# Gate weights of a low-rank expert layer spread by DMA within SBUF instead of by a matmul, with h left in PSUM

## Chip, cores and metric

One core of one Trainium2 chip runs the whole kernel. The metric is the time of one execution on the device in microseconds (us), as the median over several executions. The engines are named as in the profile: PE is TensorE's matmul side and PEld its weight loads, DVE is VectorE, ACT is ScalarE, POOL is GpSimd, SP is the engine that only issues DMAs here.

## The reference

All of it is float32. 64 batches of 64 tokens with 512 features go through a conditioned layer and then through a feed-forward layer with low-rank experts:

```
q_emb = relu(cond @ W3 + b3)                       # (64, 512)
x1    = (64 * x + sum_over_tokens(x)) * q_emb      # (64, 64, 512)  (n is x.shape[1] = 64)
y     = relu(x1 @ W2 + b2)
base  = y @ W_base + b_base
shared = (y @ A_s) @ B_s                           # rank 16
gates = softmax(y @ W_router + b_router)           # 6 experts
w     = gates where among the top 2 of the token, else 0
h     = y @ A_r                                    # per expert, rank 16
routed = sum over experts of (h * w) @ B_r
out   = x + base + shared + routed
```

## The kernel before

The 4096 tokens are cut into NG = 8 groups of TG = 512 tokens (TT = 4 tiles of 128 tokens; KC = 4 chunks of 128 features). Every large product is made in three passes of a format with fewer bits: each operand is split into hi and lo, and hi*hi, hi*lo and lo*hi are added up in PSUM (`product`, L658 to L663, whose matmuls all carry L661).

For a group there are these stages. **Turn and total** (DVE): the load in quarters x_quart is transposed to xT (`turn_x`, L420), summed over the tokens of a batch (`sum_x`, L426) and added (`add_sum`, L432). POOL multiplies by q_emb (`scale`, L277) into x1_full, ACT rounds to x1_hi (`x1_split`, L318) and DVE makes x1_lo (`x1_rest`, L443). **m1** (PE, L665): four outputs of 12 matmuls, y before the relu. ACT makes y_full and y_hi (`relu`, L323), DVE y_lo (`y_rest`, L449). **h** (PE, L705): 12 matmuls into the PSUM bank hT. One product gives all low-rank rows at once: rows 0 to 5 are the router's logits, row 6 (ONE) is empty and gets its 1 from a bias, rows 16 to 31 (SH) are the shared expert's, rows 32 to 127 (RO on) are 6 experts x 16. **m2** (PE, L719): 48 matmuls of y with W_base into four banks m2_ps, tokens on partitions. **Gates**: ACT copies the logits' rows out of hT (h_head, L394) and evacuates all of hT with its bias to h_sb (L398); DVE turns the logits so that tokens stand on partitions, and ranks the experts (`rank_experts`, L476); ACT takes the exponential; DVE divides the two largest by the sum (`gates`, L505) and transposes the result back (wT, L522). **Expand**: ACT copies wT's four quarters to the four diagonal blocks of w_quads (`w_spread`, L359 to L364), and one matmul with the constant 0/1 matrix pick writes, over h in the bank hT, the weight of each row and token (`expand`, L742 to L748). So that the weights lose nothing in the format with fewer bits, w_pack holds each of them as hi and lo in two columns (L516 to L520), and pick adds the two; a column of ones feeds the rows 0 to 31. DVE multiplies (`weigh`, L524 to L532): hw_full = hT * h_sb. ACT rounds to hw_hi (`hw_split`, L366) and DVE makes hw_lo (`hw_rest`, L534). **up** (PE, L729): 12 matmuls of hw with B into the four banks of m2; DVE adds x (`add_x`, L540, instructions at L548) and SP stores.

The order of each engine is written out by hand in a `step(g, par)` for each, the groups interleaved; semaphores alone tie the engines together. PE (L759 on): in step g >= 1 expand(g-1), m1 of outputs 0 and 1, up for group g-1, m1 of outputs 2 and 3, then h and m2 of group g. In the last step expand(7) stands before the last three products of m2, and up in two halves follows. DVE (L551 on): in a step g >= 2 it turns chunk 0 of group g+1, then weigh(g-1), total of chunk 0, hw_rest, y_rest(0) and so on, and near the end rank_experts(g), gates(g) and the last two x1_rest. In the first two steps the order differs: turn(3) and total(3) stand behind gates. The first step g=0 uses `m1_first` (L678). In the last step weigh, hw_split and hw_rest run over halves of 256 tokens.

h of the next group waits until weigh has read hT (`hw_ready`, L711 to L712). weigh waits for h_ready (h_sb) and gates_done (expand); expand waits for h_ready and for w_quads_ready.

SP's queue in step g (L231 to L239) is: wait until the four chunks of group g are turned, load the quarters of group g+2 (L205); store the four tiles of group g-1 as each becomes ready (L229); load x_nat of group g+1 (L239). ACT and POOL issue no DMA in the steps.

The semaphore count that the gates use is GATE_STEPS = 11 a group. Before the steps, POOL builds w_pack's zeros, w_quads' zeros and pick_one (L263 to L275), and ACT copies pick_one to the four blocks of pick (L355 to L357), behind the rounding of W_base and ahead of the first relu.

## Time and profile before

| what | value |
|---|---|
| median of 3 runs | 247.85 us (246.45 to 248.17) |
| the profiled execution | 246.59 us |
| its span, first to last instruction | 244.9 us |
| mean granted TensorE clock in it | 0.979 of full speed |

The profile is of one execution. Its span is what all stretches and waits below are parts of; the time around it is the rest up to 246.59 us. A time in a row is counted from the start of the span.

### The profile page before, as it was taken

How to read it: one execution, taken by the hardware profiler on the slowest of the kernel's cores; microseconds unless marked ns; L12 is line 12 of the kernel's file. 1: busy time of each engine (PE TensorE's matmuls, PEld its weight loads, DVE VectorE, ACT ScalarE, POOL GpSimd, SP SyncE). 2: the span in 40 equal slices, each digit the busy share in tenths (PEclk: the TensorE clock that was granted, in tenths of full speed). 3: DMA queues.
4: the chain of work that ended last, by engine and by line, in shares of the span. 5: the costliest groups of instructions: out<-in, count | busy, mean ns of one | idle time of the engine just before them, and what ended most of it. 6: DMA issues, size and time to landing. Idle time of an engine off the chain costs nothing.

```text
span 244.9 us, 3159 instructions
## 1 busy us (share of the span) xinstructions
PE 235.0 (96%) x1007; PEld 189.4 (77%) x1007; DVE 177.4 (72%) x324; ACT 102.1 (42%) x206; POOL 55.7 (23%) x58
## 2 busy tenths in 40 slices
PE   7699599999999999999999999999999999999994
PEld 2577378888887878888888888888888888888883
DVE  0697898869988996679766995679756995351344
ACT  2247557234434445245533455145433455134330
POOL 5078971202312041012302121012202121000000
PEclk9769979999999999999999999999999999999999
DMA  7989990818016368019610567018000530013004
GB/s 151 299 198 208 270 249 1 170 69 280 0 58 116 146 200 171 0 43 299 143 33 0 183 197 137 0 43 300 0 0 0 192 150 0 0 53 120 3 0 173
DMA packets 32219, 28.49 MB, mean 116 GB/s; under 512 B 6173, under 2 KB 22621, under 8 KB 32206
## 3 DMA queue, kind: packets, MB, share of 16 engines
q1 hardware_dynamic: 32050, 28.33, 42.9%
q8 instruction: 6, 0.10, 0.2%
q14 instruction: 7, 0.06, 0.1%
q10 hardware_dynamic: 156, 0.00, 0.0%
HBM read 19.94 MB, written 8.39 MB: 116 GB/s over the span
## 4 chain that ended last, share of the span: by engine, by line
PE 69%; DVE 16%; SPq 6%; DMA 4%; issue 2%; POOL 1%; ACT 1%; POOLq 0%; DVEq 0%
PE m_ps L661 61%; PE hT L661 7%; DMA x_quart<-in_x_dram 4%; DVE xT L424 4%; DVE out_nat L548 3%; DVE x_sum L438 3%; SPq L217 2%; DVE vsum L429 2%; DVE y_lo L452 2%; SPq L205 1%; POOL x_full L284 1%; DVE x_lo L446 1%; SPq L211 1%; PE hT L748 1%; ACT x_hi L321 1%
## 5 line engine op out<-in xcount | busy, mean ns | idle before, releaser
L284 POOL TENSOR_TENSOR x_full<-x_sum,qT 128x512 f32<-128x512 f32 x31 | 37.9, 1222 | 138.5 <-DVE x_sum L438 138.5
L661 PE MATMUL m_ps<-Wb_lo,y_hi 128*128 128x512 f32 x128 | 50.1, 391 | 0.0
L661 PE MATMUL m_ps<-Wb_hi,y_lo 128*128 128x512 f32 x128 | 50.1, 391 | 0.0
L661 PE MATMUL m_ps<-Wb_hi,y_hi 128*128 128x512 f32 x128 | 50.0, 391 | 0.0
L661 PE MATMUL m_ps<-x_hi,W_hi 128*128 128x512 f32 x112 | 43.8, 391 | 0.2 <-DVE x_lo L446 0.2
L661 PE MATMUL m_ps<-x_lo,W_hi 128*128 128x512 f32 x112 | 43.6, 389 | 0.0
L661 PE MATMUL m_ps<-x_hi,W_lo 128*128 128x512 f32 x112 | 43.6, 389 | 0.0
L329 ACT ACTIVATE y_full<-m_ps,b_sb 128x512 f32<-128x512 f32 x32 | 22.0, 688 | 49.3 <-PE m_ps L661 46.4
L424 DVE STREAM_TRANSPOSE xT<-x_quart 128x512 f32<-128x512 f32 x32 | 34.8, 1088 | 7.6 <-DMA x_quart<-in_x_dram 7.6
L452 DVE TENSOR_TENSOR y_lo<-y_full,y_hi 128x512 fp32r<-128x512 f32 x32 | 25.0, 780 | 12.5 <-ACT y_hi L331 12.5
L446 DVE TENSOR_TENSOR x_lo<-x_full,x_hi 128x512 fp32r<-128x512 f32 x32 | 22.9, 719 | 10.9 <-ACT x_hi L321 10.9
L321 ACT ACTIVATE x_hi<-x_full 128x512 fp32r<-128x512 f32 x32 | 20.1, 632 | 22.2 <-POOL x_full L284 21.4
L661 PEld LDWEIGHTS m_ps<-Wb_hi,y_hi 128*128 128x128 f32 x128 | 24.3, 190 | 5.0
L661 PEld LDWEIGHTS m_ps<-Wb_lo,y_hi 128*128 128x128 f32 x128 | 24.2, 189 | 5.1
L661 PEld LDWEIGHTS m_ps<-Wb_hi,y_lo 128*128 128x128 f32 x128 | 24.2, 189 | 5.1
L438 DVE SCALAR_TENSOR_TENSOR x_sum<-xT,vsum 128x512 f32<-128x512 f32 x32 | 24.8, 774 | 2.1
L661 PEld LDWEIGHTS m_ps<-x_hi,W_hi 128*128 128x128 f32 x112 | 21.0, 188 | 5.2 <-DVE x_lo L446 0.9
L548 DVE TENSOR_TENSOR out_nat<-m_ps,x_nat 128x512 f32<-128x512 f32 x32 | 20.6, 683 | 5.5 <-PE m_ps L661 5.5
L661 PEld LDWEIGHTS m_ps<-x_hi,W_lo 128*128 128x128 f32 x112 | 21.0, 188 | 4.4
L661 PEld LDWEIGHTS m_ps<-x_lo,W_hi 128*128 128x128 f32 x112 | 21.0, 188 | 4.3
L429 DVE TENSOR_REDUCE vsum<-xT 128x8 f32<-128x512 f32 x32 | 21.8, 680 | 0.3
L331 ACT ACTIVATE y_hi<-m_ps,b_sb 128x512 fp32r<-128x512 f32 x32 | 21.8, 682 | 0.0
(82 smaller groups left out, 263.7 us busy)
## 6 DMA issues: line engine op xcount, KB each, us to landing
x_quart<-in_x_dram SPq DMA_DIRECT2D x32, 256.0 KB, 4.8
x_nat<-in_x_dram SPq DMA_DIRECT2D x8, 1024.0 KB, 6.0
out_dram<-out_nat SPq DMA_DIRECT2D x32, 256.0 KB, 2.1
W_f<-in_L_cond_W_dram SPq DMA_DIRECT2D x4, 256.0 KB, 6.3
Wb_f<-in_L_ffn_W_base_dram SPq DMA_DIRECT2D x1, 1024.0 KB, 7.0
W_sb<-in_L_cond_W_dram SPq DMA_DIRECT2D x1, 512.0 KB, 6.0
Wd_f<-in_L_ffn_A_r_dram SPq DMA_DIRECT2D x4, 48.0 KB, 3.1
Wu_f<-in_L_ffn_B_r_dram SPq DMA_DIRECT2D x1, 192.0 KB
```

The source lines that it names most:

```text
L217: sp.dma_start(Wd_f[:, k, RO:P].rearrange("p (e r) -> p e r", r=R), A_r[:, k * P:(k + 1) * P, :].rearrange("e p r -> p e r")).then_inc(Wd_ ...
L284: nc.gpsimd.tensor_tensor(per_batch(x1_full[:, c, :]), per_batch(x1_sum[:, c, :]), qT[:, c, bass.ds(BG * g, BG)].unsqueeze(2).to_broadcast ...
L321: nc.scalar.activation(x1_hi[par][:, c, :], x1_full[:, c, :], ACT.Copy).then_inc(x1_hi_ready, 1)
L329: nc.scalar.activation(y_full[m % 2][:, :], m1_ps[m][:, :], ACT.Relu, bias=b2_sb[:, m:m + 1]).then_inc(y_full_ready, 1)
L331: nc.scalar.activation(y_hi[:, m, :], m1_ps[m][:, :], ACT.Relu, bias=b2_sb[:, m:m + 1]).then_inc(y_hi_ready, 1)
L424: nc.vector.transpose(xT[c % 2][:, :], x_quart[par][:, :, :].rearrange("p b (i c) -> p c b i", c=KC)[:, c]).then_inc(xT_ready, 1)
L429: nc.vector.tensor_reduce(vsum[c % 2][:, :], per_batch(xT[c % 2][:, :]), AX.X, ALU.add).then_inc(vsum_ready, 1)
L438: nc.vector.scalar_tensor_tensor(out=per_batch(x1_sum[:, c, :]), in0=per_batch(xT[c % 2][:, :]), scalar=float(N), in1=vsum[c % 2][:, :].un ...
L446: nc.vector.tensor_tensor(x1_lo[par][:, c, :], x1_full[:, c, :], x1_hi[par][:, c, :].bitcast(F32), ALU.subtract).then_inc(x1_lo_ready, 1)
L452: nc.vector.tensor_tensor(y_lo[:, m, :], y_full[m % 2][:, :], y_hi[:, m, :].bitcast(F32), ALU.subtract).then_inc(y_lo_ready, 1)
L548: nc.vector.tensor_tensor(out_nat[par][:, t, :], m2_ps[t][:, :], x_nat[par][:, t, :], ALU.add).then_inc(out_ready, 1)
L661: mm = nc.tensor.matmul(psum, lhsT, rhs, start=start and i == 0, stop=stop and i == len(terms) - 1)
```

## The change

The weights reach the rows of h without TensorE. DVE writes them once, in float32, to w_nat (no hi and lo, no column of ones) and transposes to wT as before. SP then issues four DMAs, one for each quarter of the tokens, from six partitions of wT to the 96 partitions 32 to 127 of the new tile gatesT, each source row read 16 times. Rows 0 to 31 of gatesT are set to 1.0 once by POOL. In SP's step the four issues stand last, behind a wait for wT, so ahead of the next step's load of quarters. `weigh` waits for all four and adds the bias and multiplies in one instruction, hw_full = (hT + h_bias) * gatesT, reading h from PSUM; h_sb is gone, and so are w_full, the hi/lo packing, w_quads, pick, expand and what built them. GATE_STEPS is 9. The diff, without most of the declarations:

```diff
-        w_full = sb("w_full", [P, TT, E])
-        w_pack = sb("w_pack", [P, TT, S], F32R)
+        w_nat = sb("w_nat", [P, TT, S])
...
-        w_quads = sb("w_quads", [P, TG], F32R)
-        pick_one = sb("pick_one", [S, P])
-        pick = sb("pick", [P, P], F32R)
+        gatesT = sb("gatesT", [P, TG])
...
-        GATE_STEPS = 11
+        GATE_STEPS = 9
 
         block = ctx.enter_context(nc.Block())
 
@@ -237,6 +232,10 @@
                     store(g - 1, 1 - par)
                 if not (isinstance(g, int) and g + 1 >= NG):
                     sp.dma_start(x_nat[1 - par][:, :, :], at(x_groups, g + 1)).then_inc(x_loaded[1 - par], 16)
+                sp.wait_ge(wT_ready, g + 1)
+                for q in range(NQ):
+                    spread = wT[q * S:q * S + E, :].unsqueeze(1).to_broadcast([E, R, P])
+                    sp.dma_start(gatesT[RO:P, q * P:(q + 1) * P], spread).then_inc(gates_spread, 16)
 
             step(0, 0, first=True)
             with sp.Fori(0, (NG - 4) // 2) as pair:
@@ -260,19 +259,8 @@
 
             nc.gpsimd.affine_select(out=earlier[:, :, :], in_=earlier[:, :, :], compare_op=ALU.is_gt, fill=0.0,
                                     base=0, pattern=[[1, E], [-1, E]], channel_multiplier=0).then_inc(const_ready, 1)
-            nc.gpsimd.memset(w_pack[:, :, :].bitcast(F32), 0.0).then_inc(pick_step, 1)
-            nc.gpsimd.memset(pick_one[:, :], 0.0).then_inc(pick_step, 1)
-            nc.gpsimd.memset(w_quads[:, :].bitcast(F32), 0.0).then_inc(const_ready, 1)
-            pool.wait_ge(pick_step, 2)
-            nc.gpsimd.memset(w_pack[:, :, 2 * E:2 * E + 1].bitcast(F32), 1.0).then_inc(const_ready, 1)
-            experts = pick_one[:, RO:P].rearrange("p (e r) -> p e r", r=R)
-            nc.gpsimd.affine_select(out=experts, in_=experts, compare_op=ALU.not_equal, fill=1.0,
-                                    base=0, pattern=[[-1, E], [0, R]], channel_multiplier=1).then_inc(pick_step, 1)
-            nc.gpsimd.affine_select(out=pick_one[:, 0:RO], in_=pick_one[:, 0:RO], compare_op=ALU.not_equal, fill=1.0,
-                                    base=-2 * E, pattern=[[0, RO]], channel_multiplier=1).then_inc(pick_step, 1)
-            pool.wait_ge(pick_step, 4)
-            nc.gpsimd.affine_select(out=experts, in_=experts, compare_op=ALU.not_equal, fill=1.0,
-                                    base=-E, pattern=[[-1, E], [0, R]], channel_multiplier=1).then_inc(pick_step, 1)
+            nc.gpsimd.memset(w_nat[:, :, :], 0.0).then_inc(const_ready, 1)
+            nc.gpsimd.memset(gatesT[0:RO, :], 1.0).then_inc(const_ready, 1)
 
             def scale(g, c):
 
@@ -352,17 +340,6 @@
             act.wait_ge(b2_loaded, 16)
             act.wait_ge(bias_loaded, 16)
 
-            act.wait_ge(pick_step, 5)
-            for q in range(NQ):
-                nc.scalar.activation(pick[q * S:(q + 1) * S, :], pick_one[:, :], ACT.Copy).then_inc(pick_ready, 1)
-
-            def w_spread(g):
-
-                act.wait_ge(wT_ready, g + 1)
-                for q in range(NQ):
-                    nc.scalar.activation(w_quads[q * S:(q + 1) * S, q * P:(q + 1) * P], wT[q * S:(q + 1) * S, :],
-                                         ACT.Copy).then_inc(w_quads_ready, 1)
-
             def hw_split(toks, n):
 
                 act.wait_ge(hw_ready, n)
@@ -393,9 +370,6 @@
                 for q in range(NQ):
                     nc.scalar.activation(h_head[q * S:(q + 1) * S, :], hT[0:S, q * P:(q + 1) * P], ACT.Identity,
                                          bias=h_bias[0:S, 0:1]).then_inc(h_head_ready, 1)
-                if not first:
-                    act.wait_ge(hw_ready, g)
-                nc.scalar.activation(h_sb[:, :], hT[:, :], ACT.Identity, bias=h_bias[:, 0:1]).then_inc(h_ready, 1)
                 if first:
                     split(0)
                     split(1)
@@ -405,7 +379,6 @@
                 nc.scalar.activation(expo[:, :, :], logit[:, :, :], ACT.Exp).then_inc(expo_ready, 1)
                 if first:
                     split(2)
-                w_spread(g)
                 split(3)
                 if last:
                     hw_split(slice(0, TG // 2), g + 1)
@@ -513,13 +486,9 @@
                 nc.vector.reciprocal(rden[:, :], den[:, :]).then_inc(gate_step, 1)
                 dve.wait_ge(gate_step, done + 9)
                 top, norm = expo_top[:, :, :], rden[:, :].unsqueeze(2).to_broadcast([P, TT, E])
-                nc.vector.tensor_tensor(w_full[:, :, :], top, norm, ALU.mult).then_inc(gate_step, 1)
-                nc.vector.tensor_tensor(w_pack[:, :, 0:E], top, norm, ALU.mult).then_inc(gate_step, 1)
-                dve.wait_ge(gate_step, done + 11)
-                nc.vector.tensor_tensor(w_pack[:, :, E:2 * E], w_full[:, :, :], w_pack[:, :, 0:E].bitcast(F32),
-                                        ALU.subtract).then_inc(w_ready, 1)
+                nc.vector.tensor_tensor(w_nat[:, :, 0:E], top, norm, ALU.mult).then_inc(w_ready, 1)
                 dve.wait_ge(w_ready, g + 1)
-                nc.vector.transpose(wT[:, :], w_pack[:, :, :].bitcast(F32).rearrange("p t j -> p (t j)")).then_inc(wT_ready, 1)
+                nc.vector.transpose(wT[:, :], w_nat[:, :, :].rearrange("p t j -> p (t j)")).then_inc(wT_ready, 1)
 
             def weigh(g, toks, n):
 
@@ -527,9 +496,9 @@
                     dve.wait_ge(hw_hi_ready, g)
                 if isinstance(g, int) and g == NG - 1:
                     dve.wait_ge(hw_hi_ready, NG - 1)
-                dve.wait_ge(h_ready, g + 1)
-                dve.wait_ge(gates_done, g + 1)
-                nc.vector.tensor_tensor(hw_full[:, toks], hT[:, toks], h_sb[:, toks], ALU.mult).then_inc(hw_ready, 1)
+                dve.wait_ge(gates_spread, 16 * NQ * (g + 1))
+                nc.vector.scalar_tensor_tensor(out=hw_full[:, toks], in0=hT[:, toks], scalar=h_bias[:, 0:1],
+                                               in1=gatesT[:, toks], op0=ALU.add, op1=ALU.mult).then_inc(hw_ready, 1)
 
             def hw_rest(toks, n):
 
@@ -739,14 +708,6 @@
                     product(m2_ps[t][:, :], [(hw_lo[:, toks], Wu_hi[:, :])], False, True).then_inc(m2_done, 1)
 
 
-            def expand(g):
-
-                if isinstance(g, int) and g == 0:
-                    pe.wait_ge(pick_ready, NQ)
-                pe.wait_ge(h_ready, g + 1)
-                pe.wait_ge(w_quads_ready, NQ * (g + 1))
-                nc.tensor.matmul(hT[:, :], pick[:, :], w_quads[:, :], start=True, stop=True).then_inc(gates_done, 1)
-
             pe.wait_ge(W3_loaded, 16)
             pe.wait_ge(condT_copied, 1)
             for c in range(KC):
@@ -761,7 +722,6 @@
                 if first:
                     m1_first()
                 else:
-                    expand(g - 1)
                     m1(g, par, 0)
                     m1(g, par, 1)
                     up(range(TT), g)
@@ -790,7 +750,6 @@
 
                     for t, k in others[:-3]:
                         m2(t, k, first)
-                    expand(g)
                     for t, k in others[-3:]:
                         m2(t, k, first)
                     up(range(TT // 2), g + 1)
```

## Rows read from the trace of the kernel before

**Rows 1.** Page, part 1: busy us (share of the span) xinstructions of each engine

```profile
PE 235.0 (96%) x1007; PEld 189.4 (77%) x1007; DVE 177.4 (72%) x324; ACT 102.1 (42%) x206; POOL 55.7 (23%) x58
```

**Rows 2.** Waits of all engines: who waited for whom, us in total, times, longest

```profile
DVE hw_full L532 <- PE hT L748: 9.9, 6, 2.9
...
PE hT L661 <- DVE y_lo L452: 2.9, 2, 2.7
```

**Rows 3.** Windows: stretch, length, busy us of each engine, granted clock, DMA share

```profile
core 0: us, PE busy (x) PEld busy (x) DVE busy (x) ACT busy (x) POOL busy (x), PEclk, DMA share, GB/s
30.40:33.50 3.10, 3.10 (x7) 2.46 (x8) 3.10 (x5) 2.65 (x5) 2.52 (x2) 0.50 1.20 215
45.30:72.70 27.40, 27.40 (x122) 22.52 (x121) 23.98 (x41) 11.48 (x23) 3.94 (x4) 1.00 0.40 111
72.70:101.20 28.50, 28.04 (x123) 22.56 (x122) 23.29 (x43) 12.11 (x24) 5.85 (x5) 1.00 0.57 145
```

**Rows 4.** Chain that ended last, in order of time: start us, us, what

```profile
101.51 13.60 PE m_ps L661 x60
```

**Rows 5.** Groups by form: line engine op out<-in shapes xcount | busy, mean ns | idle before

```profile
L438 DVE SCALAR_TENSOR_TENSOR x_sum<-xT,vsum 128x512 f32<-128x512 f32 x32 | 24.8, 774 | 2.1
...
L532 DVE TENSOR_TENSOR hw_full<-hT,h_sb 128x512 f32<-128x512 f32 x7 | 4.8, 685 | 7.0 <-PE hT L748 7.0
...
L748 PE MATMUL hT<-w_quads,pick 128*128 128x512 f32 x8 | 3.1, 389 | 0.0
```

**Rows 6.** Timeline of the last step: start us, us, engine, line, op, out<-in [idle before]

```profile
233.00 0.18 DVE L516 TENSOR_TENSOR w_full<-expo_top,rden 128x24 f32<-128x24 f32 x1
...
233.10 0.18 DVE L517 TENSOR_TENSOR w_pack<-expo_top,rden 128x24 fp32r<-128x24 f32 x1
...
233.31 0.18 DVE L519 TENSOR_TENSOR w_pack<-w_full,w_pack 128x24 fp32r<-128x24 f32 x1
...
233.53 0.31 DVE L522 STREAM_TRANSPOSE wT<-w_pack 128x128 f32<-128x128 f32 x1
...
236.74 0.76 DVE L532 TENSOR_TENSOR hw_full<-hT,h_sb 128x256 f32<-128x256 f32 x2 [2.89 <-PE hT L748]
...
237.19 0.75 ACT L369 ACTIVATE hw_hi<-hw_full 128x256 fp32r<-128x256 f32 x2 [2.01 <-DVE hw_full L532]
...
237.64 0.76 DVE L537 TENSOR_TENSOR hw_lo<-hw_full,hw_hi 128x256 fp32r<-128x256 f32 x2 [0.15 <-ACT hw_hi L369]
...
238.48 0.39 PE L661 MATMUL m_ps<-Wu_hi,hw_hi 128*128 128x512 f32 x1
```

**Rows 7.** Timeline of PE at the two places where it stopped in step 2

```profile
74.66 0.39 PE L661 MATMUL m_ps<-x_hi,W_lo 128*128 128x512 f32 x1
75.27 0.50 PE L661 MATMUL m_ps<-x_hi,W_hi 128*128 128x512 f32 x1 [0.22 <-DVE x_lo L446]
...
90.59 0.39 PE L661 MATMUL hT<-y_hi,Wd_lo 128*128 128x512 f32 x1
91.22 0.50 PE L661 MATMUL hT<-y_lo,Wd_hi 128*128 128x512 f32 x1 [0.24 <-DVE y_lo L452]
```

**Rows 8.** Timeline of a steady step, from wT to the first matmul of up

```profile
178.69 0.32 DVE L522 STREAM_TRANSPOSE wT<-w_pack 128x128 f32<-128x128 f32 x1
...
183.92 0.69 DVE L532 TENSOR_TENSOR hw_full<-hT,h_sb 128x512 f32<-128x512 f32 x1 [1.21 <-PE hT L748]
...
185.94 0.68 DVE L537 TENSOR_TENSOR hw_lo<-hw_full,hw_hi 128x512 fp32r<-128x512 f32 x1
...
189.06 0.39 PE L661 MATMUL m_ps<-Wu_hi,hw_hi 128*128 128x512 f32 x1
```

**Rows 9.** SP's DMA issues: timeline of one; landing times of L229, then of L205

```profile
43.14 1.94 SPq L205 DMA_DIRECT2D x_quart<-in_x_dram  x4
...
DMA to landing us min/median/max: 2.0/2.1/2.6
...
DMA to landing us min/median/max: 3.0/4.8/10.5
```

**Rows 10.** Page, part 3: DMA queue, kind: packets, MB, share of 16 engines

```profile
q1 hardware_dynamic: 32050, 28.33, 42.9%
```

More of the change, by code:

```diff
@@ L79, in adaln_ffn @@
         y_lo = sb("y_lo", [P, KC, TG], F32R)
-        h_sb = sb("h_sb", [P, TG])
         h_head = sb("h_head", [P, P])
@@ L154, in adaln_ffn @@
         m1_done, y_full_ready, y_hi_ready, y_lo_ready = sem("m1_done"), sem("y_full_ready"), sem("y_hi_ready"), sem("y_lo_ready")
-        h_done, h_ready = sem("h_done"), sem("h_ready")
+        h_done = sem("h_done")
         h_head_ready, logit_ready, expo_ready, gate_step = sem("h_head_ready"), sem("logit_ready"), sem("expo_ready"), sem("gate_step")
-        w_ready, wT_ready, w_quads_ready, gates_done = sem("w_ready"), sem("wT_ready"), sem("w_quads_ready"), sem("gates_done")
-        pick_step, pick_ready = sem("pick_step"), sem("pick_ready")
+        w_ready, wT_ready, gates_spread = sem("w_ready"), sem("wT_ready"), sem("gates_spread")
         hw_ready, hw_hi_ready, hw_lo_ready = sem("hw_ready"), sem("hw_hi_ready"), sem("hw_lo_ready")
         m2_done, out_ready = sem("m2_done"), sem("out_ready")
-        GATE_STEPS = 11
+        GATE_STEPS = 9
         block = ctx.enter_context(nc.Block())
```

## The prediction, made before the changed kernel was run

> **What bounds the kernel now.** I read the busy line of the page first, then the waits, then the stages in windows, the chain, and last the timeline at the three places where the change bites. TensorE is busy for 96% of the span [rows 1]. Of the waits that stop it the largest in the steps are two on y_lo, 2.9 us together with 2.7 in one of them [rows 2]. The long one lies near 27 to 30 us, before the first expand. In the windows of the steps, TensorE is busy for 27.40 of 27.40 us in step 1 and for 28.04 of 28.50 in step 2 [rows 3]. From there on the chain is one unbroken run of matmuls: 60 in 13.60 us, 0.227 us from start to start [rows 4]. (The 389 ns of one matmul in the groups is its length in the pipeline, not its price.) A full step is 48 matmuls of m1, 12 of up, 12 of h, 48 of m2 and one expand: 121 x 0.227 = 27.4 us, which is what the window of step 1 shows. So from about 33 us to 239 us the time is the number of matmuls times 0.227, plus small stalls in step 2. VectorE (72%) and ScalarE (42%) count only where TensorE waits for them.
>
> **What the change takes from TensorE.** Eight expand matmuls, one for each group [rows 5]: 8 x 0.227 = 1.81 us. Seven stand at the head of a step and one in the last step among the last products of m2. All lie on the path, for nothing stops the engine before or behind them.
>
> **What it takes from VectorE.** gates loses w_full and the subtraction into w_pack. In the last step w_full starts at 233.00, the multiply at 233.10, the subtraction at 233.31 and the transpose to wT at 233.53 [rows 6]: 0.10 + 0.22 = 0.32 us. In steady steps this is hidden, since VectorE idles on its own (hw_full waited 9.9 us for expand in all, in 6 of 9 cases [rows 2]). It pays in steps 1 and 2. There VectorE is nearly full (23.98 of 27.40, 23.29 of 28.50 us [rows 3]), and TensorE twice ran into it: at 75.27 for x_lo and at 91.22 for y_lo [rows 7]; counted from the matmul before each, they are 0.38 and 0.40 us beyond the pace of 0.227. By 91 us, TensorE without expand(0) and expand(1) would be 0.45 us earlier. VectorE would start its full stretch in step 1 earlier by the one expand (0.23), since its additions wait there for TensorE's up, and then save 0.32 in that step: 0.55. The two move by almost the same, so the stalls stay, shorter by about 0.1. I count 0.1 for these and 0.05 for the small stall of step 1, 0.15 in all. Bounds: 0.45 lost, if VectorE's chain doesn't move at all; about 0.8 gained, if both stalls go.
>
> The new weigh adds the bias and multiplies in one instruction, reading PSUM and SBUF as before. The multiply took 685 ns at 128x512; the same kind of two-operation instruction, x_sum, took 774 on average with its slower cases beside GpSimd [rows 5]. I take 0.69, no cost; the high end is 0.09 us a step, in step 2 alone on the path.
>
> **What it takes from ScalarE and GpSimd.** Four copies w_quads and the copy h_sb in each step, and at the start the four copies to pick. Nothing of it sets the end: ScalarE is idle for more than half of each step [rows 3]. It lets x_hi of chunk 3, which stood behind w_quads, start earlier. In steady steps VectorE then reaches weigh earlier, where it waits for gates anyway. The copies to pick are hidden by the long wait: y_lo(0) stands on VectorE behind the turn of the second group, whose input lands late, and that landing is untouched. GpSimd's shorter preamble lies before its first wait for work. I count zero, bounds 0 and 0.3 gained.
>
> **What it adds: four transfers a step on SP, and weigh waits for all of them.** The old steady case: wT starts at 178.69 and ends near 179.0, weigh starts at 183.92, the second half of the split ends at 186.62, and up wants its first operand at 189.06 [rows 8]. So the gates could come almost 3 us later than 183.92 and TensorE would still not wait. Four issues on SP took 1.94 us [rows 9]; a transfer lands in 2.1 us (the stores, 2.0 to 2.6) or 4.8 us (the loads of quarters, 3.0 to 10.5) [rows 9]. With the last issue 1.5 us after the first and 2.1 to 4.8 to landing, the gates are there 3.8 to 6.5 us after wT, at 182.5 to 185.2. Both ends are in time for up; at the near end weigh even starts earlier than before. Behind the waiting weigh stand total, hw_rest and y_rest(0) on VectorE; total feeds GpSimd and ScalarE for the next group, a step ahead of its use, and hw_rest is the split that up waits for, already counted. Cost: zero in seven steps.
>
> The transfers stand on SP behind the stores and x_nat of the same step, which are issued long before. What they move back is the next load of quarters: its issue now comes after wT and four issues instead of after the last turn, so by rank_experts and gates later, some 4 us, plus 2 for the issues; the turn that wants it stands a step of 27 us after. Hidden. The one that was issued at 43.1 [rows 9] moves by less than 1 us, since wT of the first group is there before. Hidden. If the cover were gone, each microsecond of lateness would be one of VectorE's.
>
> **The last step has no such cover.** Before: wT from 233.53 to 233.84, weigh's first half at 236.74 (it waited for expand), hw_hi at 237.19 (a pair takes 0.75), hw_lo at 237.64, up at 238.48 [rows 6], with TensorE never idle. After, on the same clock: wT is ready at 233.52; the first issue some 0.2 us later, the last 1.5 us behind, at 235.2. With 2.1 us to landing, weigh starts at 237.3. The old offsets (0.45 to hw_hi, about 0.42 for half a tile) give hw_hi at 238.2 and hw_lo, 0.90 + 0.42 behind weigh, at 238.6. TensorE without the last expand wants them at 238.25 and 238.70: no stall. With 4.8 us to landing the stall is 2.65. I take 2.6, the slowest store, since four stand one behind another: 0.5 us of stall.
>
> **The sum.** -1.81 (expands) - 0.15 (stalls) + 0.5 (last step) = -1.46, say -1.5 us. The profiled execution took 246.59 (span 244.9), which gives 245.1. The median of the three runs is 247.85, 1.3 above the profiled one, and the runs differ by 1.7 among themselves, as much as the whole effect. I carry the difference to the median: 246.3 us, 0.6% less. About 1% is what a measurement of this kernel can tell from no change.
>
> **Rivals.**
> (a) The last step shows no stall, the landing being 2.1 us as the stores' median: -1.96, 245.9. For it: a store moves 256 KB, a spread 96 rows of 512 B, 48 KB. Against it: four follow one another closely.
> (b) The spread runs on few DMA engines. All packets of the big queue together, 32050, took 42.9% of 16 engines' span [rows 10], so one takes 0.429 x 16 x 244.9 / 32050 = 52 ns. A spread has 96 rows of 512 B: 6 for each of 16 engines, 0.3 us, but 16 for each of six, 0.84 us. Four of them in line land at about 233.7 + 2.1 + 0.4 + 3 x 0.84 = 238.7 instead of 237.3. Then weigh is 1.4 later, TensorE stalls 1.35 us, and the sum is -1.96 + 1.35 = -0.6: 247.2. The rows don't show which engine carried which packet, so neither way is excluded; the source's outer dimension is 6 here and that of all large loads is 32 or more. The Trainium skill speaks for this rival (DMA: Bandwidth & Descriptors, "Why a DMA increments its semaphore by 16 and not by 1"): the engines used are the largest number up to 16 that divides the outermost dimension of both sides, here 6. By that rule the time would be this rival's 247.2; by sixteen engines it would be (a) or the forecast. I give it 0.2, since the 52 ns come from packets mostly larger than these.
> (c) VectorE's chain in steps 1 and 2 doesn't get shorter, and takes back the two expands (0.45) and the 0.15: -0.9, 246.95. Against it: two of its instructions are gone.
> (d) Slower: the last group's transfers land as the loads of quarters do. The last step decides, from 4.1 us to landing (2.1 without a stall plus the 1.96 saved). At 4.8 the stall is 2.65, net +0.7; and a pause of 2.7 us is what stood before the window from 30.4 to 33.5, where the granted clock was 0.50 and 7 matmuls took 3.10 us, 1.5 us more than at 0.227 [rows 2, 3]. The twelve matmuls of up would pay that again: +2.2, 250.0. At 10.5 to landing every step would pay too. Against it: the loads move 256 KB each, and no load is in flight then.
> (e) hT, held in PSUM until weigh, keeps h of the next group waiting: before, too, weigh read hT, and h waits for the same hw_ready, a good 10 us after weigh by [rows 8] and the pace; no chance of its own.
>
> **How the numbers follow.** Forecast 0.48, (a) 0.18, (b) 0.2, (c) 0.06, (d) 0.08. The differences between them are small beside the 0.7% between runs, so the range is 244.8 to 248.0: it takes in the first four cases with 1 us either side of their middle and leaves (d) out. Faster by over 1% (under 245.4): (a) and the forecast with a median that falls low, 0.18. Slower by over 1%: (d), 0.07. Within 1%: 0.75.
>
> **What would show it.** Right: steps of 120 matmuls, 27.2 us apart; no L748; weigh in steady steps idle before it for the DMA, at about 4 us after wT, and TensorE not waiting for hw_hi there. x_lo and y_lo stalls near 75 and 91 us still there. In the last step the wait of TensorE for hw_hi is the term to read: 0 for (a), 0.5, about 1.35 for (b), over 2.5 and a granted clock of 0.50 for (d). Wrong: any steady step over 27.3 us, or a wait of a turn for its quarters after 45 us.

## The result and the profile after

The changed kernel is slower: 255.38 us median (253.78 to 255.78, 4 runs) against 247.51 for the kernel before in the same runs, ratio 1.0321 (95% interval 1.029 to 1.0352). The profiled execution has a span of 253.4 us, 8.5 more than before. The forecast was 246.3 in a range up to 248.0, with 0.07 for slower.

The page first: the busy line (answers to [rows 1]), the clock's line, the queue (answers to [rows 10]) and the line of the chain by engine.

```profile
PE 237.4 (94%) x999; PEld 188.7 (74%) x999; DVE 177.9 (70%) x308; ACT 83.8 (33%) x162; POOL 54.5 (22%) x53
...
PEclk9779979999999999999999999999999999999997
...
q1 hardware_dynamic: 35314, 29.91, 45.1%
...
DVE 39%; DMA 18%; PE 16%; SPq 12%; issue 9%; ACT 4%; POOL 0%; DVEq 0%; POOLq 0%; ACTq 0%
```

The eight matmuls are gone (1007 to 999), and ScalarE has 18 us less to do. But TensorE, which carried most of the chain to the end before, holds 16% of it now. VectorE, the transfers and SP's issues have taken its place. The queue has 3264 packets more, which is 32 transfers of 102: 96 rows and six more. In the page before, the same line of the chain had TensorE at 69%:

```profile
PE 69%; DVE 16%; SPq 6%; DMA 4%; issue 2%; POOL 1%; ACT 1%; POOLq 0%; DVEq 0%
```

The waits after (who waited for whom, us, times, longest) name the place:

```profile
DVE hw_full L500 <- DMA gatesT<-wT: 37.5, 8, 7.3
...
PE hT L630 <- DVE y_lo L425: 5.0, 6, 2.3
...
PE m_ps L630 <- ACT hw_hi L346: 3.4, 1, 3.4
```

Before, weigh had waited 9.9 us in all for the expand matmul [rows 2]. Now it waits 37.5 us for the transfers, and TensorE has new waits behind that: for y_lo in six places instead of two, and for hw_hi in the last step.

Windows after (columns as in [rows 3]): two steps, the last stretch, and within it the part in which TensorE's last matmuls run:

```profile
105.00:133.00 28.00, 27.37 (x121) 22.30 (x120) 21.22 (x38) 9.43 (x18) 4.80 (x4) 1.00 0.43 119
133.20:161.30 28.10, 27.52 (x122) 22.45 (x121) 21.21 (x38) 9.43 (x18) 4.80 (x4) 1.00 0.44 120
...
244.00:253.40 9.40, 4.29 (x12) 2.81 (x12) 4.44 (x8) 0.81 (x2) 0.00 (x0) 0.82 0.30 112
...
247.20:250.10 2.90, 2.89 (x8) 1.69 (x6) 1.75 (x3) 0.00 (x0) 0.00 (x0) 0.50 0.49 181
```

A steady step now leaves TensorE idle for half a us and more. In the last 9.4 us the granted clock is 0.82 on average, and 0.50 from 247.2 to 250.1. The timeline of VectorE and SP in one steady step (answers to [rows 8]):

```profile
126.06 0.31 DVE L491 STREAM_TRANSPOSE wT<-w_nat 128x128 f32<-128x128 f32 x1
...
127.46 1.08 DVE L397 STREAM_TRANSPOSE xT<-x_quart 128x512 f32<-128x512 f32 x1
133.90 0.75 DVE L500 SCALAR_TENSOR_TENSOR hw_full<-hT,h_bias,gatesT 128x512 f32<-128x512 f32 x1 [5.35 <-DMA gatesT<-wT]
```

```profile
126.40 3.78 SPq L238 DMA_DIRECT2D gatesT<-wT  x4
```

From wT's start to weigh are 7.8 us: before, they were 5.2 [rows 8]. Four issues take 3.78 us, not the 1.94 of the loads of quarters [rows 9]; the last begins 2.4 us after the first (not 1.5), and its transfer lands 5.1 us after that, not 2.6. What follows from it is in the chain in order of time (start, us, what):

```profile
126.06 0.32 DVE wT L491
126.40 0.81 SPq L238
...
128.80 5.07 DMA gatesT<-wT
133.90 0.08 DVE hw_full L500
...
148.71 0.58 DVE y_lo L425
149.34 0.51 PE hT L630
149.87 0.36 ACT h_head L371
```

This is a ring: h gives the gates, the gates go through SP and the DMA engines to weigh, behind weigh stand 15 us of VectorE's own work in its written order, the last of it y_lo of chunk 3, and TensorE needs that to finish the next h. Once round takes 28.1 us (121.23, 149.34, 177.40 for the same matmul of h), against 27.2 us of matmuls. TensorE can't run ahead of it.

The last step has the wait in the open (timeline, VectorE and TensorE; answers to [rows 6]):

```profile
237.24 0.31 DVE L491 STREAM_TRANSPOSE wT<-w_nat 128x128 f32<-128x128 f32 x1
244.81 0.87 DVE L500 SCALAR_TENSOR_TENSOR hw_full<-hT,h_bias,gatesT 128x256 f32<-128x256 f32 x2 [7.26 <-DMA gatesT<-wT]
```

```profile
245.79 0.50 PE L630 MATMUL m_ps<-Wu_hi,hw_hi 128*128 128x512 f32 x1 [3.37 <-ACT hw_hi L346]
246.13 0.40 PE L630 MATMUL m_ps<-Wu_lo,hw_hi 128*128 128x512 f32 x1
...
248.18 0.63 PE L630 MATMUL m_ps<-Wu_hi,hw_lo 128*128 128x512 f32 x1
248.61 0.63 PE L630 MATMUL m_ps<-Wu_hi,hw_hi 128*128 128x512 f32 x1
```

TensorE stands for 3.4 us, and the second half of its twelve matmuls starts 0.43 us apart instead of 0.227, at the granted clock of 0.50 shown above.

### The profile page after: what moved, and what is told of

The parts are those of the page before. It is cut to its first block, busy times and chain, and to the rows that moved or that the text cites. A ratio compares the mean times of both kernels' runs of the same rounds, so it can differ in the third digit from the quotient of the medians.

```text
span 253.4 us, 3088 instructions
## 1 busy us (share of the span) xinstructions
PE 237.4 (94%) x999; PEld 188.7 (74%) x999; DVE 177.9 (70%) x308; ACT 83.8 (33%) x162; POOL 54.5 (22%) x53
## 4 chain that ended last, share of the span: by engine, by line
DVE 39%; DMA 18%; PE 16%; SPq 12%; issue 9%; ACT 4%; POOL 0%; DVEq 0%; POOLq 0%; ACTq 0%
DMA gatesT<-wT 14%; PE m_ps L630 12%; DVE xT L397 7%; SPq L238 6%; DVE out_nat L517 6%; DVE y_lo L425 5%; DVE vsum L402 5%; DVE x_sum L411 4%; DMA x_quart<-in_x_dram 4%; PE hT L630 4%; ACT h_head L371 3%; SPq L212 2%; DVE x_lo L419 2%; SPq L200 1%; DVE hw_lo L506 1%
## 5 line engine op out<-in xcount | busy, mean ns | idle before, releaser
L500 DVE SCALAR_TENSOR_TENSOR hw_full<-hT,h_bias,gatesT 128x512 f32<-128x512 f32 (+1 forms) x9 | 6.1, 690 | 37.5 <-DMA gatesT<-wT 37.5
L425 DVE TENSOR_TENSOR y_lo<-y_full,y_hi 128x512 fp32r<-128x512 f32 x32 | 28.3, 883 | 5.8 <-ACT y_hi L319 5.8
L346 ACT ACTIVATE hw_hi<-hw_full 128x512 fp32r<-128x512 f32 (+1 forms) x9 | 5.2, 584 | 65.6 <-DVE hw_full L500 65.6
```

What stands on the lines that cost most here:

```text
L425: nc.vector.tensor_tensor(y_lo[:, m, :], y_full[m % 2][:, :], y_hi[:, m, :].bitcast(F32), ALU.subtract).then_inc(y_lo_ready, 1)
```

## The experiments

The theory to test, called W in the texts on record: the change's savings are real, and the wait of weigh for late transfers costs everything beyond them. Then, why the transfers are late: P, reads of neighbouring partitions hold one another up; K, six DMA engines are too few; I, the issues. One table serves all runs. The profiled span of each is cut into three parts: up to the start of wT of the first group, before which no spread is issued; from there to the start of wT of the last group, seven steps; and from there to the end. The first part differs by up to 2.4 us among runs that have the same work in it (40.35 in e2, 42.77 in e4), so it is kept apart. The column before the last gives the transfers' whole way in the last group, from wT's start to weigh's; it lies within the last part.

| run | ratio to before (95%) | first wT starts | seven steps | last wT to weigh | last wT to the end |
|---|---|---|---|---|---|
| before | 1 | 41.07 | 192.46 | 3.21 | 11.37 |
| changed | 1.0321 (1.029 to 1.0352) | 41.49 | 195.75 | 7.57 | 16.16 |
| e1 no wait | 0.9918 (0.9889 to 0.9948) | 41.08 | 190.70 | 0.23 | 11.32 |
| e2 weigh later | 1.015 (1.0108 to 1.0192) | 40.35 | 192.19 | 7.58 | 16.16 |
| e3 rows four apart | 0.9967 (0.9936 to 0.9998) | 40.86 | 190.77 | 4.97 | 12.37 |
| e4 24 rows | 0.9992 (0.9966 to 1.0019) | 42.77 | 190.89 | 5.13 | 12.54 |
| e5 rows two apart | 0.9989 (0.9972 to 1.0006) | 41.07 | 190.77 | 5.31 | 12.66 |
| e6 two queues | 0.9998 (0.9979 to 1.0017) | 40.73 | 190.77 | 5.76 | 13.10 |
| e7 four apart, two queues | 0.9937 (0.9914 to 0.9961) | 41.70 | 190.74 | 3.99 | 11.36 |
| e8 h_sb kept | 1.033 (1.0299 to 1.0361) | 41.53 | 195.70 | 7.57 | 16.27 |
| e9 two queues crossed | 1.0276 (1.0211 to 1.0341) | 40.48 | 193.25 | 7.28 | 17.07 |
| e10 32 rows | one run, 246.07 us | 41.56 | 190.87 | 4.28 | 11.67 |

One profile stands behind each row, but the way from wT to weigh repeats in every steady step of it: 7.5 to 7.9 us in the changed kernel, 4.9 to 5.0 in e3, 5.0 to 5.2 in e4, 5.2 to 5.4 in e5, 5.7 to 6.0 in e6, 7.2 to 7.4 in e9.

**e1: is it the wait at all?** The product leaves the weights out here.

```diff
-  sp.dma_start(gatesT[RO:P, q * P:(q + 1) * P], spread).then_inc(gates_spread, 16)
+  sp.dma_start(spread_T[RO:P, q * P:(q + 1) * P], spread).then_inc(gates_spread, 16)
...
-  nc.gpsimd.memset(gatesT[0:RO, :], 1.0)
+  nc.gpsimd.memset(gatesT[:, :], 1.0)
...
-  dve.wait_ge(gates_spread, 16 * NQ * (g + 1))      # in weigh
+  dve.wait_ge(gates_spread, 16 * NQ * g)            # a step later, before wT is written again
```

> The four transfers are issued as in the changed kernel, but into a tile that nobody reads; weigh multiplies with a tile that is 1.0 throughout and waits for no transfer (the gates' weights are left out of the product). Theory W (the wait for the late transfers costs it all, in VectorE's order and in the last step): the eight expand matmuls are gone and nothing stalls in their place, so the profiled span is about 243 (244.9 before, less 1.8), ratio to before about 0.992. Rival C (the transfers disturb by being there: SP's queue moved back, SBUF ports, the weigh that reads PSUM holding the bank): the time stays over 250, ratio over 1.01.

Measured: 0.9918, span 243.1, 1.8 us less than before and 10.3 less than the changed kernel. With the same transfers in flight, the same queue and the same weigh, TensorE loses nothing in a steady step (window of e1, 28.00 us of 28.00):

```profile
105.00:133.00 28.00, 28.00 (x126) 23.17 (x125) 21.21 (x40) 9.74 (x19) 4.80 (x4) 1.00 0.46 127
```

So theory W holds and rival C falls: all that the change costs comes through the wait. The 10.3 us divide by the table: 0.41 lie before the first wT, 5.05 in the seven steps (195.75 against 190.70), and 4.84 in the last step (16.16 against 11.32).

**e2: the steps' part, by VectorE's order alone.**

```diff
   turn(0)
-  weigh_before()
   total(0)
+  turn(1)
+  weigh_before()
   hw_rest_before()
   y_rest(g, 0)
-  turn(1)
```

> weigh stands 3.4 us of VectorE's work later in the steps from 2 on (after total of chunk 0 and the turn of chunk 1); transfers and last step unchanged. Theory W: the work put ahead fills VectorE's wait (4.7 us a step in the changed kernel), steps go back from 28.1 to about 27.3 us, so about 3 to 4 us of the 8.5 come back and the last step keeps its stall of 3.4 and the slow matmuls behind it: ratio to before 1.017 to 1.022. If instead up is what the late weights hold (TensorE itself waiting for hw_hi), putting weigh later makes the steps longer: ratio over 1.03.

Measured: 1.015, span 248.7, 4.7 us less than the changed kernel, a little more than forecast; 3.56 of it lie in the seven steps, inside the forecast of 3 to 4. The transfers take their 7.58 us as before and the last step costs the same 16.16. Of the steps' loss of 5.05 us 1.5 are left, all in the first two steps (28.60 and 27.59 us, against 28.15 and 26.51 in e1). Weigh stands later in VectorE's order, and in time just where it stood (7.8 to 7.9 us after wT in the middle steps of both), and the steps are shorter, so it is not up that was held: it was the work behind weigh in VectorE's order. Steady steps are back at 27.2 us (wT of two groups of e2):

```profile
123.74 0.31 DVE L491 STREAM_TRANSPOSE wT<-w_nat 128x128 f32<-128x128 f32 x1
...
150.94 0.31 DVE L491 STREAM_TRANSPOSE wT<-w_nat 128x128 f32<-128x128 f32 x1
```

**e3: why the transfers are late.** The six source rows of a quarter are put on partitions 0, 4, 8 to 20 of their 32 instead of 0 to 5.

```diff
-  spread = wT[q * S:q * S + E, :].unsqueeze(1).to_broadcast([E, R, P])
+  spread = wT[q * S:q * S + 4 * E:4, :].unsqueeze(1).to_broadcast([E, R, P])
...
-  nc.vector.tensor_tensor(w_nat[:, :, 0:E], top, norm, ALU.mult)
+  nc.vector.tensor_tensor(w_nat[:, :, 0:4 * E:4], top, norm, ALU.mult)
```

> The six source rows of a quarter lie four partitions apart instead of side by side; everything else as in the changed kernel (still six rows read 16 times, 102 packets a transfer). Theory P (the reads of neighbouring partitions hold each other up): the last group's transfers land at least 1.5 us earlier than 7.3 us after wT, ratio to before about 1.02. Theory K (the number of DMA engines is what is short, six of 16 here): no change, ratio 1.032. The Trainium skill (SBUF — State Buffer, on the DMA port swizzle) has four neighbouring partitions share one port, which would speak for P.

Measured: 0.9967, a larger gain than the 1.02 that theory P had. Weigh comes 2.6 us earlier, the steps' loss is gone (190.77 against 190.70 in e1), and of the last step's 4.84 us 1.05 are left. The number of packets is the same. The DMA view of the last group shows what changed, first the changed kernel (237.5 to 245), then e3 (231.8 to 237.5); the first line of each is the busy share of the 16 DMA engines in 40 slices, in tenths:

```profile
DMA  0000000022222232222212123322121111100000
...
DMA packets 408, 0.20 MB, mean 26 GB/s; under 512 B 24, under 2 KB 408, under 8 KB 408
...
q1 hardware_dynamic: 408, 0.20, 16.8%
```

```profile
DMA  0000000000034300144100442002440000000000
...
DMA packets 408, 0.20 MB, mean 35 GB/s; under 512 B 24, under 2 KB 408, under 8 KB 408
...
q1 hardware_dynamic: 408, 0.20, 11.6%
```

Each has 384 rows and 24 small packets, six a transfer. In the changed kernel the four transfers run into one smear; in e3 they are four short bursts with gaps between. The engines' time is 0.168 x 16 x 7.5 = 20.2 us in the one and 0.116 x 16 x 5.7 = 10.6 in the other, 49 and 26 ns a packet. The trace's record of each packet tells more. The packets of 512 B in the last group, by their time:

```
                            under 30 ns   30 to 44   45 to 59   60 and more
changed                          40         154          9         181
e3 rows four apart              384           0          0           0
e5 rows two apart                57         306         19           2
e4 24 rows                       91         281         10           2
e6 two queues                   226          81         14          63
e9 two queues crossed            83         106         25         170
e7 four apart, two queues       361          23          0           0
```

In the changed kernel they are of two kinds, slow ones of mostly 60 to 80 ns (median 69) and fast ones around 35. Six small packets a transfer fit six engines; which engine took which packet the trace doesn't say. If each of the six has one source row, 16 times, then four of them read in partitions 0 to 3 and two in 4 and 5, which would explain the two kinds. It does not explain their number: four engines with slow packets throughout would have 256 of them, and there are 181. The packets run from 238.99 to 244.39, 5.4 us. From 242.74 to 243.54 all are slow, and eight begin in each 0.2 us, one every 25 ns: three are in flight at a time, not four. So the reads do hold each other up, and how the engines share them in detail stays open.

**e4: more engines instead.** Each weight is written four times, so that 24 rows are each read four times.

```diff
-  spread = wT[q * S:q * S + E, :].unsqueeze(1).to_broadcast([E, R, P])
+  spread = wT[q * S:q * S + 4 * E, :].unsqueeze(1).to_broadcast([4 * E, R // 4, P])
```

> Each weight is written four times by VectorE, so that wT has 24 rows a quarter and each is read four times. Theory K: the transfer runs on 12 DMA engines instead of six (108 packets a transfer instead of 102), its landing comes down like the packets per engine, from 64 to 32 at 52 ns, so about 1.7 to 2.5 us earlier; ratio to before about 1.02. Theory P: the same gain, since the rows also spread over more partitions, but then the run with rows four apart shows it as well. Theory I (the four issues on SP, 3.7 us, and a fixed time to landing are what is long): under 0.7 us earlier, ratio 1.03. By the Trainium skill (DMA: Bandwidth & Descriptors, on why a DMA increments its semaphore by 16) 24 and 96 give 12 engines.

Measured: 0.9992 (expected about 1.02), weigh 5.13 us after wT. This alone can't tell K from P, and the small packets say that the engines did double (48 for four transfers, 12 each). But twice the engines did not beat six with rows apart (4.97). Most packets take 30 to 44 ns. That would fit two neighbouring rows to an engine, and so two engines at a block of four partitions, which the trace doesn't show directly. The next run has packets of the same kind on six engines, and there the two can be compared.

**e5: the dose.** Rows on partitions 0, 2, 4 to 10.

```diff
-  spread = wT[q * S:q * S + E, :].unsqueeze(1).to_broadcast([E, R, P])
+  spread = wT[q * S:q * S + 2 * E:2, :].unsqueeze(1).to_broadcast([E, R, P])
```

> The dose between the changed kernel (source rows side by side) and the run with rows four apart: rows two apart, so two of them in each block of four partitions. In the changed kernel's last group the packets fall into two kinds, 69 to 76 ns and 34 to 42 ns; with rows four apart all take 27 ns. Theory P (reads from one block of four partitions share one way out): four rows there give 69 to 76 ns, two give 34 to 42, so here all packets take 34 to 42 ns, weigh of the last group starts 4.7 to 5.3 us after wT (7.3 and 4.7 in the two others), and the ratio to before is 0.995 to 1.000. If it were the neighbourhood of partitions itself rather than the block, it would already be free here as with four apart: 27 ns. If it were the span of partitions read, between: some 5.9 us after wT, ratio 1.01.

Measured: 0.9989 as theory P had it, 5.31 us at the edge of its 4.7 to 5.3, and 306 of 384 packets at 30 to 44 ns (57 are faster). So it is how many source rows lie within four partitions that counts: one 27 ns, two about 35, four up to about 70 (the counts above). Whether the blocks begin at multiples of four, no run tells. In e4, with the same kind of packets and twice the engines, the last transfer lands 2.18 us after its issue, here 2.51, and weigh comes 0.2 us sooner there (5.13 against 5.31): that is about all that is left of theory K.

**e6: the issue.**

```diff
-  for q in range(NQ):          # SP
+  for q in range(NQ // 2):     # SP
       ...
+  act.wait_ge(wT_ready, g + 1)     # ScalarE, where w_spread stood
+  for q in range(NQ // 2, NQ):
+      act.dma_start(gatesT[RO:P, q * P:(q + 1) * P], spread).then_inc(gates_spread, 16)
```

> Of the changed kernel's four transfers two are issued by ScalarE, where w_spread stood, two by SP; source rows side by side as in the changed kernel. Theory P: the reads are the limit (64 packets of 69 to 76 ns on the slow engines, 4.8 us), so the issue counts for little: weigh of the last group at most 0.7 us earlier than 7.3 us after wT, ratio 1.02 to 1.03. Theory I (the issues, 3.7 us on one queue, are the limit): 1.5 us or more earlier, ratio 1.01.

Measured: 0.9998, weigh 1.8 us earlier. The expectation from theory P was a miss: it said 0.7 at most. Either the issue counted after all, or the two queues read over two different ways out, which the packet counts hint at (226 under 30 ns). e9 was made to tell.

**e9: the same two queues, quarters crossed.** SP issues the quarters 0 and 2, ScalarE 1 and 3. Nothing else differs from e6.

> As the run with two queues, rows side by side, but SP issues the quarters 0 and 2 and ScalarE 1 and 3 (there SP had 0 and 1, ScalarE 2 and 3). The quarters' source rows start at partitions 0, 32, 64 and 96. Theory Q (partitions 0 to 3 and 32 to 35 share a way out, 64 to 67 and 96 to 99 another, so that in the earlier run the two queues read over two different ones): now both queues read over the same one at a time, the two-queue gain of 1.8 us in the last group mostly goes, weigh starts 7.0 to 7.6 us after wT's start (5.8 there, 7.6 in the changed kernel) and the ratio to before is 1.01 to 1.03. Theory R (two queues are simply served side by side): no difference from that run, 5.8 us, ratio 1.000. The Trainium skill (SBUF — State Buffer, on the DMA port swizzle) has these four quarters on two ports in this way, which speaks for Q.

Measured: 1.0276, weigh 7.28 us after wT. The gain of two queues is all but gone, with the same number of issues on each. So the issue was not what e6 shortened, but for the 0.3 us by which e9 is ahead of the changed kernel. Quarters 0 and 1 (partitions 0 to 3 and 32 to 35) share one way out, and 2 and 3 (64 to 67, 96 to 99) another. One queue, or crossed queues, sends all readers first over the one and then over the other; e6 uses both at once. This is the port map of the Trainium skill (SBUF — State Buffer, "Door 1: The DMA port swizzle"), and here the runs agree with it: 5.76 against 7.28 us. That page gives it as a matter of bandwidth; a transfer of 48 KB shows it as latency.

Two more things stand in e9's profile. Its steps take 27.6 us, which helps to size the ring (below). And its last step is longer than the changed kernel's (17.07 against 16.16) though weigh comes 0.3 us sooner: all twelve matmuls of up run at a granted clock of 0.50, where in the changed kernel the first half still had 1.00. TensorE had stood for 3.08 us before them here and for 3.37 there, so the length of the pause alone does not say when the clock falls; that stays open.

```profile
241.90:247.50 5.60, 5.49 (x12) 3.81 (x12) 2.89 (x5) 0.44 (x2) 0.00 (x0) 0.50 0.25 94
```

**e7: both.** Rows four apart, and two queues as in e6.

> Rows four apart and two queues together. With rows four apart each transfer's data is there in one burst of half a us, the bursts 0.8 us apart, so the four issues on SP (3.1 us) have become the limit. Theory: two queues bring the last group's weigh from 4.7 to 3.1 to 3.5 us after wT, the last stall of 0.8 us (TensorE for hw_hi) goes, and the span is that of the run without a wait, 243.1 to 243.5; ratio 0.991 to 0.994. If both queues' issues go one at a time, nothing is gained over rows four apart alone: ratio 0.997.

Measured: 0.9937, weigh 3.99 us after wT. That is 1.0 us sooner than e3, though not the 3.1 to 3.5 expected. It is enough: from wT to the end takes 11.36 us, as without any wait (11.32), and the ratio is at the edge of the expected 0.991 to 0.994. With rows apart, then, the issues on one queue are a part of what is long: the last of four on SP begins 2.3 us after the first in e3, the last of two about 0.8 us after it here, and 1.0 of these 1.5 us reach weigh. This version beats both kernels, the kernel before by 0.6% (0.4 to 0.9), a small gain but one outside its interval.

**e8: is it h in PSUM?** ScalarE copies h to h_sb as before; weigh multiplies h_sb and gatesT.

```diff
+  nc.scalar.activation(h_sb[:, :], hT[:, :], ACT.Identity, bias=h_bias[:, 0:1]).then_inc(h_ready, 1)
...
-  nc.vector.scalar_tensor_tensor(out=hw_full[:, toks], in0=hT[:, toks], scalar=h_bias[:, 0:1],
-                                 in1=gatesT[:, toks], op0=ALU.add, op1=ALU.mult)
+  nc.vector.tensor_tensor(hw_full[:, toks], h_sb[:, toks], gatesT[:, toks], ALU.mult)
```

> The changed kernel with the copy h_sb back on ScalarE; weigh multiplies h_sb and gatesT, both in SBUF. Theory W: h in PSUM until weigh plays no part, the time is the changed kernel's within 0.3%: ratio 1.03. Rival C (the bias add in weigh, 751 ns instead of 685, and the read of PSUM cost in VectorE's chain): up to 0.1 us a step better, ratio 1.027 to 1.03. If the held bank were what makes TensorE's h wait, this would be clearly faster.

Measured: 1.033, the changed kernel's time. The second half of the change, h left in PSUM, costs and brings nothing that can be seen while the ring sets the pace. For the held bank e8 is no test, since TensorE's h waits for hw_ready, that is for weigh, in both versions. The changed kernel's trace answers that: weigh begins at 133.90, and the first matmul that writes hT again starts at 144.74 without waiting.

**e10: why an issue takes so long.** The rows of h get weights here that are not all the reference's.

```diff
-  spread = wT[q * S:q * S + E, :].unsqueeze(1).to_broadcast([E, R, P])
+  spread = wT[q * S:(q + 1) * S, :].unsqueeze(1).to_broadcast([S, (P - RO) // S, P])
```

> Each transfer reads 32 source rows three times instead of six 16 times (the rows of h then get weights that are not all the reference's; bytes, packets and order are the same). Question: why does one issue take 0.72 to 0.75 us, where a load of quarters took 0.36. Theory X (a transfer on fewer than 16 DMA engines costs its queue the difference): 16 engines here, 112 packets a transfer, and the issue falls to about 0.4 us, four in 1.9 us, weigh in the last group 3.7 to 4.2 us after wT's start. Theory Y (the shape, a source row repeated, or SBUF as the source costs it): 0.72 us stays, four in 3.1 us, weigh some 5 us after wT's start.

Measured in one run: the four issues take 2.50 us in the last group, and weigh comes 4.28 us after wT. SP's issues as the trace has them, e3 first, then e10, then e4 (durations of one in ns, least, median, most):

```profile
L238 SPq DMA_DIRECT2D gatesT<-wT x32: 721/724/926, 41.2 to 234.3; - x32
```

```profile
L238 SPq DMA_DIRECT2D gatesT<-wT x32: 577/598/688, 41.9 to 234.7; - x32
```

```profile
L238 SPq DMA_DIRECT2D gatesT<-wT x32: 778/788/945, 43.1 to 236.5; - x32
```

Neither theory: the issue falls, but to 598 ns and not to 400. And the number of engines doesn't order them: by the small packets e3 has six a transfer, e4 twelve and e10 sixteen, and the median issues are 724, 788 and 598 ns. What makes the issue long stays open.

## Why the prediction was wrong

The forecast was 1.5 us less, and the profiled span is 8.5 us longer: 1.8 saved, 0.4 lost before the first wT, 5.05 lost in the seven steps and 4.84 in the last.

**The savings: right.** e1 has the savings and no wait. In the seven steps it takes 1.76 us less than the kernel before (190.70 against 192.46); seven expands at 0.227 and 0.15 of stalls were to give 1.74. The whole is 1.8. That ScalarE's evacuation was worth nothing agrees with e8, though only in a kernel that the ring holds; the w_quads copies were not tried alone.

**The last step: the mechanism was right, the size was not.** The prediction put its only cost there, 0.5 us, from "2.6, the slowest store", and four issues in 1.94. By these weigh was to start 4.6 us after wT's start (at 233.2 on its clock). Measured: 7.57. The last issue began 2.34 us after the first instead of 1.5, and its transfer landed 4.78 after that instead of 2.6. The step cost 4.84 us: 3.4 of standing, and 1.4 because the twelve matmuls of up took 4.3 us from first start to last end instead of 2.9, half of them at the lower clock level. Rival (d) had this chain with its price: at 4.8 us to landing a stall of 2.65 and the slow matmuls, 250.0. It got 0.08 because "the loads move 256 KB each, and no load is in flight then": size was taken for what makes a landing late. A spread is five times smaller than a store and landed 4.8 us after its issue, a store 2.1.

**Rival (b) had half of the cause.** The transfers do run on six engines, so far as the small packets show it: 102 packets, six of them small. But the price was worked out with an average packet (52 ns) spread evenly, 64 in line. The average was right, 52 ns for the packets of 512 B, and the even spread was not: 181 of 384 took 60 ns and more, with source rows side by side, and the last transfer landed 4.8 us after its issue. With rows apart and again six small packets a transfer they land 2.6 us earlier (e3), with 12 engines no sooner than that (e4).

**The steady steps: the step of the prediction that failed.** "Cost: zero in seven steps" was 5.05 us. It rested on two things. One is the landing: 3.8 to 6.5 us after wT was allowed, and it was 7.8. The other is the deadline. The prediction measured weigh against up and found room for almost 3 us beyond 183.92, that is until some 8 us after wT; by this deadline even 7.8 was free. It dismissed what stands behind weigh on VectorE because it feeds the next group "a step ahead of its use". But the four y_rest stand there too, and h of the same step needs the last of them. e2 separates the two: with weigh at the same time after wT but less work behind it, the steady steps are back at 27.2.

The true deadline can be worked out. Where TensorE waits for y_lo, so that the ring sets the pace, a step is the way from wT to weigh and a rest that does not change: 28.09 with 7.84 and 27.79 with 7.52 in the changed kernel, 27.62 with 7.36 and 27.45 with 7.18 in e9. The rest is 20.25 to 20.27 us in all four. TensorE's own 27.2 us leave 6.9 for the way from wT to weigh, an estimate from these rows. In e6, with 5.7 to 6.0, the steps are 27.2. So a landing within the 6.5 that the prediction allowed would have cost nothing in the steps; and with the right landing but the wrong deadline of 8, the forecast would still have been zero. It took both terms to see this cost.

VectorE at 72% busy looked as if it had room. It has, but before weigh: its idle time lies at the waits, and behind weigh there are 15 us without a gap to speak of.

The prediction's own mark was the right one to look at: "any steady step over 27.3 us" would show it wrong, and they were 28.1.

## What to carry to other kernels

A transfer within SBUF that carries a result from one engine to another is priced by its whole way, issues and landing, and by which partitions it reads: a few neighbouring rows read many times were the slowest case measured here, and spreading the same rows over the partitions cost nothing and took 2.6 us off. The deadline of a wait on an in-order engine is not that of the instruction that waits but of every instruction behind it; follow them until another engine needs one of them, and see whether the path closes to a ring. Independent work put before the wait opens such a ring without a shorter transfer (e2); where nothing independent is left, as in the last step, only the shorter way helps (e3, e7).

## What the runs showed of the hardware that was not expected

Packets of 512 B read from SBUF took 27 ns where one source row lay within four partitions (e3), about 35 with two (e5), and with four up to 60 to 80 (changed kernel, 181 of 384). The times of e6 and e9 (5.76 and 7.28 us) fit together if rows 32 partitions apart within one half share a way out and the halves don't. An issue on SP took 0.72 us for six source rows to 96, 0.79 for 24 rows (e4) and 0.60 for 32 (e10); in the same kernels a store took 0.34. Where the packets were slow, the last of the four issues stretched, to as much as 1.39 us, and the four together took 3.74 us instead of 3.07 (changed kernel against e3).
